# Cross-attention and low-rank FFN on one core: values on half chunks of 64 keys, and the output projection moved between the scores and the values

## What is computed

```python
q = layernorm(x) @ Wq + bq                       # 16 heads of 32
k, v = ctx @ Wk + bk, ctx @ Wv + bv              # 77 keys
attn = softmax(clip(q @ k.T * 32 ** -0.5, -1e4, 1e4))
x = x + (attn @ v) @ Wo + bo
H = gelu((layernorm(x) @ U1) @ V1 + b1)          # 512 -> 128 -> 2048
x = x + (H @ U2) @ V2 + b2                       # 2048 -> 128 -> 512
```

## Time and profile before

| | us |
|---|---|
| three runs, median (range) | 610.06 (609.22 to 610.79) |
| the profiled execution, its own time | 610.8 |
| its span, first to last instruction | 608.9 |
| PE busy | 581.9 (96%) |
| DVE busy | 488.9 (80%) |
| POOL busy | 358.1 (59%) |
| ACT busy | 309.6 (51%) |
| attention, from the first scores to the last values | about 30 to 360 |

### The profile page before, as it was taken

The page is one execution under the profiler, slowest core; times in us unless marked ns, Lnnn a source line. Parts: engine busy times, 40 slices in busy tenths (PEclk is TensorE's granted clock), DMA queues, the critical chain, the costliest instruction groups (busy, mean ns, idle before and its releaser), DMA issues.

```text
span 608.9 us, 11499 instructions
## 1 busy us (share of the span) xinstructions
PE 581.9 (96%) x4583; PEld 478.9 (79%) x4583; DVE 488.9 (80%) x706; ACT 309.6 (51%) x505; POOL 358.1 (59%) x250
## 2 busy tenths in 40 slices
PE   6988899999999999999999897999999999999996
PEld 5786888888888888888886666878888888888884
DVE  3489878797879787988768986697979797978675
ACT  1435254445444444444445553565757575757562
POOL 2548575657565756675666535565656665656561
PEclk8989899999999999999999999999999999999999
DMA  8423064122312221222122134003030302001012
GB/s 263 153 66 110 20 211 142 39 97 88 104 40 84 87 105 47 78 87 71 53 104 71 53 122 172 2 18 122 34 104 36 104 36 103 36 36 52 18 52 86
DMA packets 29746, 50.31 MB, mean 83 GB/s; under 512 B 5069, under 2 KB 6783, under 8 KB 29567
## 3 DMA queue, kind: packets, MB, share of 16 engines
q1 hardware_dynamic: 29215, 48.80, 23.6%
q10 hardware_dynamic: 480, 0.80, 0.6%
HBM read 32.49 MB, written 16.78 MB: 81 GB/s over the span
## 4 chain that ended last, share of the span: by engine, by line
PE 78%; DVE 9%; DMA 4%; ACT 3%; issue 2%; POOL 2%; SPq 1%; DVEq 0%; ACTq 0%; POOLq 0%
PE bank L922 44%; PE ps_s L922 14%; PE bank L1019 6%; PE bank L996 5%; PE ps_s L970 4%; PE bank L1043 2%; DVE ssum L723 2%; PE bank L944 2%; DMA fw<-in_L_xattn_Wk 2%; DVE smax L718 1%; DMA xs<-in_x 1%; DMA fw<-y_between 1%; DVE ss L709 1%; PE ps_s L1087 1%; DVE once L762 1%
## 5 line engine op out<-in xcount | busy, mean ns | idle before, releaser
L454 POOL TENSOR_TENSOR hs_r<-ss,hs_r 128x512 fp32r<-128x512 f32 x63 | 89.7, 1424 | 93.2 <-ACT hs_r L622 92.7
L601 ACT ACTIVATE ss<-ps_s,bias_c 128x512 f32<-128x512 f32 x128 | 88.1, 689 | 69.3 <-PE ps_s L922 65.7
L387 POOL TENSOR_TENSOR ss<-ss,smax 128x1232 f32<-128x1232 f32 x32 | 75.0, 2344 | 70.7 <-DVE smax L718 70.7
L922 PE MATMUL ps_s<-p1t_r,v_r 128*128 128x512 f32 x384 | 113.3, 404 | 0.6 <-DVE p1t_r L774 0.6
L922 PE MATMUL bank<-hs_r,u_r 128*128 128x512 f32 x384 | 110.2, 396 | 1.4 <-DVE hs_r L785 1.4
L922 PE MATMUL bank<-zt_r,wqo_r 128*128 128x256 f32 x768 | 100.7, 287 | 0.4 <-DVE zt_r L661 0.4
L922 PE MATMUL bank<-wqo_r,ot_r 128*128 128x512 f32 x384 | 97.7, 403 | 0.2 <-DVE xs L741 0.2
L922 PEld LDWEIGHTS bank<-zt_r,wqo_r 128*128 128x128 f32 x768 | 94.5, 191 | 1.6 <-issue 1.0
L394 POOL TENSOR_TENSOR ss<-ss,rsum 128x1232 f32<-128x1232 f32 x32 | 72.1, 2252 | 39.2 <-DVE rsum L725 39.2
L922 PEld LDWEIGHTS bank<-hs_r,u_r 128*128 128x128 f32 x384 | 72.4, 189 | 19.3 <-DVE hs_r L785 2.3
L922 PEld LDWEIGHTS ps_s<-p1t_r,v_r 128*128 128x128 f32 x384 | 70.6, 190 | 15.6 <-DVE v_r L748 1.1
(11 more groups left out here) (89 smaller groups left out, 855.6 us busy)
## 6 DMA issues: line engine op xcount, KB each, us to landing
xs<-in_x SPq DMA_DIRECT2D x64, 256.0 KB, 3.1
y_between<-xs SPq DMA_DIRECT2D x32, 256.0 KB, 2.0
xs<-y_between SPq DMA_DIRECT2D x4, 1024.0 KB, 5.5
fw<-y_between SPq DMA_DIRECT2D x4, 1024.0 KB, 5.4
out<-xs SPq DMA_DIRECT2D x16, 256.0 KB, 2.0
out<-fw SPq DMA_DIRECT2D x16, 256.0 KB, 2.0
ss<-in_L_xattn_Wq SPq DMA_DIRECT2D x2, 512.0 KB, 10.8
xs<-in_L_xattn_Wo SPq DMA_DIRECT2D x1, 1024.0 KB, 11.0
```

Source lines behind the costliest of these rows:

```text
L387: pool.tensor_tensor(heads(sc, k), heads(sc, k), smax[:, k, :].unsqueeze(2).broadcast_to([P, H, KV]), ALU.subtract).then_inc(s_sub, 1)
L454: pool.tensor_tensor(hs[:, c % 4, 1, :], hg[:, c % 4, :], hs[:, c % 4, 0, :].bitcast(F32), ALU.subtract)\
L601: act.activation(hg[:, c % 4, :], ps_s[:, c % 4, :], ACT.Gelu_apprx_tanh, bias=b1_c[:, c:c + 1]).then_inc(h_gelu, 1)
L922: mm = pe.matmul(ps, lhs(a), rhs(c), start=first and i == 0, stop=last and i == len(PASSES) - 1)
```

## The change

**Values.** Each head's first 64 keys now fill half a chunk: chunk c (0 to 7) has head 2c in rows 0 to 63 and head 2c + 1 in rows 64 to 127. The last 16 keys of every head (three of them again, with value rows of zero) fill chunks 8 and 9, four heads to a half chunk. A product takes one half of 64 rows, so PE works on two row tiles by four column tiles. There are 32 products (64 MATMULs), eight to each bank and e, and each of the eight tiles has four products. Row tile r writes bank B5 or B6, both banks are written to the end, and `pv_full` is signalled once, after the last product. The matmuls wait for `zt_lo` before all of them, not before the second half.

**Probabilities.** `normalise` now writes to a second buffer `sn` (two tiles), in two POOL instructions: 16 x 64 columns and 16 x 16 columns. `ss` holds two tiles of scores and two of `sn`. `clip` waits for `s_norm` of the tile two places earlier, `normalise` for the transposes of the tile two places earlier. The zero columns go, and the first GELU waits for the last `s_norm`.

**Order.** project_out(n-2, 0) moves ahead of turn_probs(n-1, 0), right behind scores(n, 0). project_out(n-2, 1) moves behind turn_z(n+2), right ahead of weigh_values(n-1). DVE's `y_sum` of u = 1 moves behind `turned_z`, ahead of `sums` of u = 1.

**Placement.** Two transfers of 64 rows x 512 columns and eight of 13 rows take the place of the 25.

```diff
-        ss = sb("ss", [P, 4 * NCH * P])
-        sc = ss[:, :].rearrange("p (s w) -> p s w", s=4)
+        ss = sb("ss", [P, 2 * HKV + 2 * NCH * P])
+        sc = ss[:, 0:2 * HKV].rearrange("p (s w) -> p s w", s=2)
+        sn = ss[:, 2 * HKV:].rearrange("p (s w) -> p s w", s=2)
...
-        vrows = sb("vrows", [P, B, NP, DH])
+        vrows = sb("vrows", [P, 2, B, 2, GH, DH])
...
             def normalise(j, b, u):
-                k = 2 * b + u
-                pool.wait_ge(s_rec, 2 * num(j, b) + u + 1)
-                pool.tensor_tensor(heads(sc, k), heads(sc, k),
-                                   rsum[:, k, :].unsqueeze(2).broadcast_to([P, H, KV]),
+                k, s = 2 * b + u, 2 * num(j, b) + u
+                pool.wait_ge(s_rec, s + 1)
+                until(pool, pt_full, 3 * (s - 1))
+                pool.tensor_tensor(sn[:, u, 0:H * HALF].rearrange("p (h w) -> p h w", h=H), heads(u)[:, :, 0:HALF],
+                                   rsum[:, k, :].unsqueeze(2).broadcast_to([P, H, HALF]), ALU.mult)
+                grouped = lambda t: t.rearrange("p (i g) w -> p i g w", i=GH)
+                pool.tensor_tensor(sn[:, u, H * HALF:].rearrange("p (g i w) -> p i g w", g=G, i=GH),
+                                   grouped(heads(u)[:, :, KV - TAIL:KV]),
+                                   grouped(rsum[:, k, :].unsqueeze(2).broadcast_to([P, H, TAIL])),
                                    ALU.mult).then_inc(s_norm, 1)
...
             def heads_high(j, b):
                 n = 2 * j + b
+                act.wait_ge(pv_full, n + 1)
                 for half, bk_ in ((0, B5), (1, B6)):
-                    act.wait_ge(pv_full, 2 * n + half + 1)
-                    act.activation(ot[:, 0, 2 * half:2 * half + 2, :],
-                                   bk_[:, :].rearrange("p (g t) -> p g t", g=2), ACT.Copy).then_inc(ot_hi, 1)
+                    act.activation(ot[:, 0, half::2, :],
+                                   bk_[:, :].rearrange("p (e t) -> p e t", e=2), ACT.Copy).then_inc(ot_hi, 1)
...
             def clip(j, b, u):
...
-                until(dve, pt_full, 3 * (s - 3))
-                dve.tensor_scalar(sc[:, k, 0:HKV].rearrange("p (g w) -> p g w", g=G), ps_s[:, :, 0:GW],
+                until(dve, s_norm, s - 1)
+                dve.tensor_scalar(sc[:, u, :].rearrange("p (g w) -> p g w", g=G), ps_s[:, :, 0:GW],
...
             def weigh_values(j, b):
 
                 n = 2 * j + b
                 pe.wait_ge(pt_copied, 6 * n + 6)
-                for half, bk_ in ((0, B5), (1, B6)):
-
-                    if half and (not isinstance(j, int) or n + 3 < NA):
-                        pe.wait_ge(zt_lo, 2 * (n + 3) + 1)
-                    for i in range(2):
-                        for head, q, c, first, final in value_steps(2 * half + i):
-                            d0 = head * DH
-                            last = pe.matmul(bk_[d0:d0 + DH, i * TA:(i + 1) * TA], vrows[:, b, q, :],
-                                             pt[:, c, :], start=first, stop=final)
-                    last.then_inc(pv_full, 1)
+                if there(NA, j, b, 3):
+                    pe.wait_ge(zt_lo, 2 * (n + 3) + 1)
+                for e in range(2):
+                    for part in range(2):
+                        for i in range(GH):
+                            c = 2 * GH + e if part else 2 * i + e
+                            for r, bk_ in ((0, B5), (1, B6)):
+                                rows = slice(r * HALF, (r + 1) * HALF)
+                                last = pe.matmul(bk_[i * DH:(i + 1) * DH, e * TA:(e + 1) * TA],
+                                                 vrows[rows, part, b, e, i, :], pt[rows, c, :],
+                                                 start=part == 0, stop=part == 1)
+                last.then_inc(pv_full, 1)
```

More of the change, by code:

```diff
@@ L27 @@
 SCALE = DH ** -0.5
[L29 to L37, removed]
+HALF = P // 2
+TAIL = HALF // GH
 TA = 256
@@ L270, in _ @@
             sp.wait_ge(zeroed, 1)
[L271 to L276, removed]
+            for r in range(2):
+                sp.dma_start(vrows[r * HALF:(r + 1) * HALF, 0, :, :, :, :].rearrange("p b e i d -> p (b e i d)"),
+                             v_f[0:HALF, r, :, :, :].rearrange("p b e d -> p (b e d)")).then_inc(v_placed, 16)
+            load_x(2, 0)
+            v_heads = v_f.rearrange("p r b e (i d) -> p r (b e) i d", i=GH)
+            for r in range(2):
+                for i in range(GH):
+                    p0 = r * HALF + (i + 1) * TAIL - (KV - HALF)
+                    sp.dma_start(vrows[p0:p0 + KV - HALF, 1, :, :, i, :].rearrange("p b e d -> p (b e) d"),
+                                 v_heads[HALF:KV, r, :, i, :]).then_inc(v_placed, 16)
             def load_ffn():
@@ L371, in _ @@
             rstd_of(0, 0)
[L372 removed]
+            pool.memset(vrows[:, 1, :, :, :, :], 0.0).then_inc(zeroed, 1)
             pool.wait_ge(wq_hi, 2)
@@ L594, in gelu @@
                 act.wait_ge(h_full, n + 1)
+                if is_block(0, j, b) and c == 0:
+                    act.wait_ge(s_norm, 2 * NA)
                 if not isinstance(j, int) or n >= 4:
@@ L838, in body @@
                             ffn_low(2)
-                        if there(NA, j, b, -2):
-                            y_sum(j - 1, b, u)
+                        if u == 0 and there(NA, j, b, -2):
+                            y_sum(j - 1, b, 0)
                         if is_block(NA, j, b) and u == 0:
@@ L850, in body @@
                         turned_z(j + 1, b)
+                    if there(NA, j, b, -2):
+                        y_sum(j - 1, b, 1)
                     if is_block(NA - 1, j, b):
@@ L1130, in body @@
                             scores(j, b, u)
+                        if u == 0 and there(NA, j, b, -2):
+                            if is_block(2, j, b):
+                                pe.wait_ge(wo_lo, 1)
+                                pe.wait_ge(zt_lo, 8)
+                            project_out(j - 1, b, 0)
                         if before:
-                            if isinstance(j, int) and num(j, b, -1) == 0 and u == 0:
-                                pe.wait_ge(pad_zero, 1)
                             turn_probs(*shift(j, b, -1), u, (0, 1))
@@ L1143, in body @@
                             turn_probs(*shift(j, b, -1), u, (2,))
-                        if there(NA, j, b, -2):
-                            if isinstance(j, int) and num(j, b, -2) == 0 and u == 0:
-                                pe.wait_ge(wo_lo, 1)
-                                pe.wait_ge(zt_lo, 8)
-                            project_out(j - 1, b, u)
                         if is_block(NA, j, b) and u == 0:
@@ L1156, in body @@
                         turn_z(j + 1, b)
+                    if there(NA, j, b, -2):
+                        project_out(j - 1, b, 1)
                     if is_block(NA - 1, j, b):
```

53 lines of the change are left out of this document (21 added, 32 removed).

## The result

| | before | after |
|---|---|---|
| runs, median (range), us | 610.42 (609.22 to 611.39), 4 runs | 617.23 (613.39 to 620.99), 4 runs |
| profiled execution, own time | 610.8 | 613.39 |
| its span | 608.9 | 611.6 |
| PE busy | 581.9 (96%) | 563.3 (92%) |
| POOL busy | 358.1 | 365.2 |

The ratio is 1.0108, 95% interval 1.0071 to 1.0144: the kernel got slower by 1.1%. PE is busy for 18.6 us less, and the end comes later all the same. The profiled execution is the fastest of the four: the median is 3.8 us above it.

What follows compares the result with a forecast made beforehand. PE was taken to bound the kernel (78% of the span). Savings of 2.6 + 0.5 + 0.3 + 0.3 = 3.7 us took the profiled 610.8 to 607.1; the median, 0.7 lower, gave 606.4, range 603.5 to 613.

Steps and rivals of the forecast that it cites:

- Values 1.90: Values stage of a block: 3.15 us become 1.90, with eight tiles of 8 MATMULs each running at once.
- single pace: Rival, chance 0.15: values go at the scores' 0.033 us per MATMUL, take 2.12, total 609.5, no change that counts.
- halves in turn: Rival, chance 0.09: row halves on one column tile cannot run together, values take 3.63, total 631.
- The wait of 1.05 behind the scores: Ahead of each block's first output projection: PE waits 1.05 us for copies and subtractions, where it waited 0.04.
- the rival in which y_sum comes late: Rival, chance 0.10: y_sum, sums or ACT's exponent come 0.5 late, each block loses its 0.24, total about 610.
- 1.05 + 2.81: Terms of the block sum behind the first scores: 1.05 us of wait, then 2.81 for the output projection.
- The second wait of 0.28: Inside turn_z: its second tile waits 0.28 us for the query half's copies, standstill start included.
- 19.84: Steady block: sum of its pieces and waits, 19.84 us against 20.08, 0.24 less.
- Block 2 gains 0.3: Early attention stage: scores 0.7 late, 0.28 second wait, values 1.25 shorter, so block 2 gains 0.3 us.
- Together 0.3 less: End of the attention stage, from block 15: later clip, delayed FFN projection and shorter last values together save 0.3 us.
- DVE's string covers most of that: Stage end: DVE's work hides most of the delay from the output projection ahead of the first FFN projection; 0.2 taken.
- The clock: Rival, chance 0.06: waits make the granted clock fall, about 1.7 us each, ten making 623; forecast held them safe.

Runs made afterwards that it cites:

- l: Changed kernel with turn_z split around the second output projection, first query half right behind the scores, block 6's tokens loaded ahead of the FFN weights: 590.52 us, ratio 0.9675.
- a: Changed kernel with the first output projection back behind part 2 of the transposed probabilities: 606.26 us, ratio 0.9916.
- b: Changed kernel with turn_z's two tiles parted by the second output projection, ACT's and DVE's work following: 611.21 us, ratio 1.0005.
- e: Changed kernel with both repairs: first output projection back behind part 2 and turn_z split around the second: 600.41 us, ratio 0.9840.
- i: Changed kernel with the first output projection behind part 2 of the transposes in the last two attention blocks only: 614.43 us, ratio 1.0062.
- j: Changed kernel with block 6's tokens loaded ahead of the FFN weights on the SP queue: 616.37 us, ratio 1.0089.
- h: Changed kernel once more, untouched, six runs for its spread: 616.97 us (613.26 to 618.98), ratio 1.0093.

## Why the prediction was wrong

The prediction was 606.4 with a range of 603.5 to 613; 617.2 was measured, on the other side of no change. The span was to get 3.7 us shorter and got 2.7 longer in the profiled execution, and the median lies 3.8 above that execution. Of the 6.4 between forecast and profile the ten steady blocks are 5.2, block 3 is 1.3, block 14 is 0.3 and the tail is 2.5; the first blocks come out 0.4 better than forecast (the first scores start that much earlier), and the FFN, with no part in the change, happened to be 2.4 shorter, which is luck.

- **Values 1.90.** Right: 1.89. Eight tiles run at once. The rivals "single pace" and "halves in turn" fall. The rule of the Trainium skill (page TensorEngine Tiling (Array Packing), section "PSUM Bottleneck") had the better sign: by it the block gains nothing, and the wait for the emptying of PSUM, with its run-in, takes 1.29 where the values give 1.25. But the same copies cost nothing in l, where queries cover them, so it is the place of the projection that lets them through. One working falls short: the weight loads of the scores were put at 0.109 each, and in the trace they last 0.181 to 0.187, so the pace of the scores is not explained by it.
- **The wait of 1.05 behind the scores.** Its idle time is right, 1.02. DVE was free in time, as reckoned: it stood idle for 0.27 ahead of its first `ot_r` part, forecast 0.24. This is not the rival in which y_sum comes late.
- **"1.05 + 2.81", the step that failed.** I added idle times, which run from an end to a start, to durations from the chain, which run from an end to an end. The run-in of the first matmul is in neither. Measured 3.08 for 2.81: **+0.27** a block. The rows to see it were there: the earlier trace rows has 3.05 for the same twelve matmuls, 2.81.
- **The second wait of 0.28 "with a start from standstill".** The same failure, and the hand-over from ACT to PE too short: the copies end and are handed over 1.01 after the queries (0.02 + 0.85 + 0.14), not 0.91. From the queries' end to the end of turn_z 1.64, forecast 0.22 + 0.87 + 0.28 = 1.37, **+0.27**. The four transposes take 0.63 there, and 0.44 behind other PE work.
- **Block.** 19.84 + 0.27 + 0.27 and 0.02 of small terms are the 20.40. Ten blocks (4 to 13) were to gain 2.4 and lost 2.8: 5.2 of the miss. a and b take one wait away each, 0.57 and 0.53, and e both, 1.10: this part is shown.
- **The first blocks.** "Block 2 gains 0.3" was thought out for the output projection; that the values in block 1 wait 1.93 for `zt_lo` was missed, since I had checked that wait in the steady block alone. Blocks 1 and 2 come out 0.4 shorter together, so the wait changed place. That the projection started at 64.14, forecast 64.3, is luck: DVE's string was 0.14 later by 54.8, not 0.9, and the values came late by their wait and a stretch at the low clock (granted 0.60 over 58 to 62). Executions with the same code up to there differ: the two blocks take 43.3 in the first profile, 42.7 in i and 44.1 in j. Block 3 loses 1.0, or much more when the tokens come late; this was nowhere in my sum. There PE's cover was the half of the values that did not need the z copies, and I let it go without a price.
- **Block 14 and POOL.** Block 14 gains 0.23 and not 0.52. POOL's multiplication is as forecast and hidden in the steady blocks: PE's timeline has no wait for `s_norm` there.
- **The tail.** "Together 0.3 less" was 2.2 more; i shows 1.9 of it to be the place of the projection. The step that failed is "DVE's string covers most of that": DVE stood still for 3.69.
- **The clock.** In the steady blocks it stayed at full in the profiles, as forecast: a wait of 1.02 did no harm. The medians lie some 4 us above the best runs of the changed kernel, and its six runs in h get longer in the main as the mean clock falls. It is not all of it: four runs of i at 0.992 lie between 611.67 and 615.73. One road to it is shown, the late tokens of block 3. j closes that road and gains nothing in the median, so the rest of these 4 us stays open. Several of the other low stretches begin at waits of about 2 us for DVE in blocks 1, 2 and 15; no run takes these waits away by themselves.

## What to carry to other kernels

A wait on the engine that bounds costs its idle time plus the run-in of the next instruction: take idle times with start-to-end durations, or end-to-end ones with a run-in added, and never mix the two. When a stage gets shorter, look at what it covered: here 1.25 us less of values uncovered the copies behind it and the z copies ahead of it, and the whole of the gain came only with a piece of work that needs neither (the queries) behind the scores. Undoing the moves that opened the waits gave 0.8 of it. A semaphore that moves from the middle of a stage to its head has to be priced where its releaser is latest, here in the first blocks, and with every transfer on the queue that leads to it.

## What the runs showed of the hardware

- Eight tiles of 64 rows by 32 columns run side by side. The window 203.85 to 203.94 holds the starts of eight matmuls, and 64 of them take 1.89 us, 0.030 each:

```profile
203.88 0.45 PE L1010 MATMUL bank<-pt,vrows 64*32 64x256 f32 x8
```

- Filling PE's idle time with other matmuls does not shorten the projection behind it: 3.07 from start to end with, 3.08 without.
- In two executions of the same kernel the same load of tokens, behind the same four loads of weights, was issued at 89.85 and at 92.67 us (one of the four took 3.53 and 6.01 us on the queue) and kept DVE waiting for 4.24 and 6.62 us. With the low clock that came with it, block 3 got 3.6 us longer.
- The granted clock can begin to fall within a wait of 3.23 us; waits of about 2 us had a low stretch behind them in some executions and none in others, at the same place of the program. Waits of 1.0 us in each block of 20.4 us left it at full in the steady blocks of every profile.
